# VectorE's order around the masked rows of the second graph

## Chip, cores and metric

One core of a Trainium2 chip runs the kernel. The metric is the device time of one execution in microseconds (us). Three runs of the kernel before gave 1057.75, 1055.41 and 1055.34 us, median 1055.41.

## The reference

For 32 batches `x` (256 channels by 512 nodes) two graph layers follow each other, each with a residual and a layer norm:

- Layer 0: two projections of `x` give a query and a key for each node; the softmax of the leaky ReLU of their sums is the attention; `agg = x @ att^T`, then `relu(adj @ agg + bias)`, added to `x`, and a layer norm over the last axis gives `h`.
- Layer 1, on rows of `h`: `z_l = h W_lang^T` and `z_g = h W_grav^T`. One 256 by 256 matrix is `A_l = max(zn zn^T, 0)` with normed rows `zn`, without its diagonal; the other is `A_g = exp(-d2 / 2 sigma^2)` with the squared distances of the rows of `z_g`. `adj` stands as the mask of both: `K_l = A_l * mask / row sums`, `K_g` likewise. `out = (w K_l + (1 - w) K_g) (h W_V^T) W_O^T`, added to `h`, and a second layer norm.

## The kernel before

The 32 batches are taken in 16 pairs. A step of the main loop has three pairs in flight: layer 1 of pair p, layer 0 of pair q = p + 1, and the projections of `x` (the x products) of pair r = p + 2. Two set-up steps come first (`early`); in the last two of the sixteen main steps no new pair comes in (`new` is false). Every engine has its own program, in which the order of the work is written out by hand, and the engines meet at semaphores only: `wait_ge` holds the engine, and all that stands behind it in its program, until a count is reached.

Matrices are kept as two float16 parts, `_hi` (made by ACT, a rounded copy) and `_lo` (made by VectorE or GpSimd, what the rounding left), and each product is three matmuls per 128 rows of contraction: hi by hi, hi by lo, lo by hi (L254 to L256). Products go to eight PSUM banks.

The part of a step that the change touches runs as follows.

- TensorE (`step`, from L509): x products 0, 1 and 2 (`wx_product`), into banks 0, 1 and 2; then `add_transposed(0)` and `(1)`, sixteen matmuls of 128 columns that add the transposed halves of the language similarity in banks 4 and 5; `norm_rows`, which spreads the inverse norms of the rows over bank 3 (semaphore `r_mm`); x products 3, 4 and 5, again into banks 0, 1 and 2; `add_transposed(2)`; x products 6 and 7 (banks 0 and 1); `add_transposed(3)`; the value products `v_product(0)` (bank 2), `(1)` (bank 0) and `(2)` (bank 1), `turn_k` for both batches, `v_product(3)` and the output products.
- An x product from the fourth on waits until the bank is read: `wx_product(k)` waits for `xw_lo` tile k - 3 (L504). Likewise `v_product(0)` waits for xw_lo tile 5, `(1)` for tile 6 and `(2)` for tile 7 (L453).
- ACT copies each x product to `xw_hi` (L616) as soon as it is there.
- VectorE makes `xw_lo` of each tile (`xw_lo_tile`: a copy of two columns at L909, then a subtraction of 256 columns at L910), and among these tiles it does other work in a fixed order: after tiles 0, 1 and 2 comes `t_lo_tile(3)` (L1069); then `masked_rows`, which for both batches of the pair multiplies the rows of bank 3 by the mask, two operations of 256 columns for each (L1102); then xw_lo tiles 3, 4 and 5; then `a_l_tiles` (L1111), which multiply the masked rows by the similarity and sum them up; `a_g_tile`, tiles 6 and 7, the sums of degrees and the K tiles (L1139).
- GpSimd makes the `h_lo` tiles (L1272) after `t_lo_tile(3)`, and SP sends them through a transposing DMA for the next step.

Of the kernel before, what the change touches and what calls it, by code (L numbers as in the profile page):

```python
# [27 lines left out]
ALU = mybir.AluOpType  # L28
# [23 lines left out]
def build(nc, x, adj, adjT, wqk, bm, wl, wg, wv, woT, gate, sigma, out):  # L52
# [4 lines left out]
    CC, OC, NC, DC = C // P, O // P, N // P, D // P  # L57
# [5 lines left out]
    with ExitStack() as ctx:  # L63
        def sb(name, shape, dt=F32):
            return ctx.enter_context(nc.sbuf_tensor(name, [P, *shape], dt))

        def sem(name):
            return ctx.enter_context(nc.semaphore(name))
# [6 lines left out]
        mask = sb("mask", [OC, O])  # L75
# [50 lines left out]
        a_l, a_g = sb("a_l", [2, OC, O]), sb("a_g", [2, OC, O])  # L126
# [13 lines left out]
        halves = [b[:].rearrange("p (c n) -> p c n", c=2) for b in bank]  # L140
# [9 lines left out]
        def wx_bank(p, k):  # L150

            return bank[late[k % 4] if p < 0 else k % 3]
# [31 lines left out]
        s = {n: sem(n) for n in names}  # L184
# [582 lines left out]
        def _(dve):  # L767
# [138 lines left out]
            def xw_lo_tile(p, k):  # L906
                r = p + 2
                dve.wait_ge(s["xw_hi_done"], 8 * r + k + 1)
                dve.tensor_copy(qk[:, k, :], wx_bank(p, k)[:, O:OW])  # L909
                dve.tensor_tensor(xw_lo[:, k // NC, k % NC, 0:O], wx_bank(p, k)[:, 0:O],  # L910
                                  xw_hi[:, k // NC, k % NC, 0:O], ALU.subtract).then_inc(s["xw_lo_done"], 1)
# [124 lines left out]
            def step(p, l0, new):  # L1036
# [28 lines left out]
                def t_lo_tile(k):  # L1065
                    dve.wait_ge(s["t_hi_done"], 4 * p + k + 1)
                    if k >= 2:
                        dve.wait_ge(s["shift_done"], 2 * p + k - 1)
                    dve.scalar_tensor_tensor(out=t_lo[:, k], in0=halves[4 + k] if k < 2 else a_g[:, k - 2],  # L1069
                                             scalar=2.0 ** -6, in1=t_hi[:, k],  # L1070
                                             op0=ALU.mult, op1=ALU.subtract).then_inc(s["t_lo_done"], 1)
# [23 lines left out]
                                                        accum_out=deg_g[:, k:k + 1])  # L1095
                    last.then_inc(s["ag_done"], 1)

                def masked_rows():
                    dve.wait_ge(s["r_mm"], p + 1)
                    for j in range(2):  # L1100
                        for c in range(OC):
                            last = dve.tensor_tensor(a_l[:, j, c, :], halves[3][:, j, :], mask[:, c, :], ALU.mult)  # L1102
                        last.then_inc(s["mr_done"], 1)

                def a_l_tiles():
                    for k in range(4):

                        j, c = k // 2, k % 2
                        dve.wait_ge(s["s_mm"], 4 * p + j + 1)
                        dve.wait_ge(s["mr_done"], 2 * p + j + 1)  # L1110
                        last = dve.scalar_tensor_tensor(out=a_l[:, j, c, :], in0=halves[4 + j][:, c, :], scalar=0.0,  # L1111
                                                        in1=a_l[:, j, c, :], op0=ALU.max, op1=ALU.mult,
                                                        accum_out=deg_l[:, k:k + 1])
                    last.then_inc(s["al_done"], 1)
# [103 lines left out]
                if new:  # L1218
                    for k in range(3):
                        xw_lo_tile(p, k)  # L1220
                t_lo_tile(3)
                masked_rows()
                if new:
                    for k in range(3, 6):
                        xw_lo_tile(p, k)
                a_l_tiles()
                a_g_tile(0)
                if new:
# [16 lines left out]

            setup0()
            pipeline(step)
            for k in range(4):
                o_stat_tile(PAIRS - 1, k)
# [107 lines left out]
```

## Time and profile before

| what | value |
|---|---|
| profiled execution, its own time | 1057.68 us |
| its span | 1056.0 us |
| median of the three runs | 1055.41 us |
| TensorE busy | 1022.2 us (97%) |
| VectorE busy | 793.9 us (75%) |
| ACT busy | 658.3 us (62%) |
| GpSimd busy | 386.2 us (37%) |
| mean granted TensorE clock | 0.991 |

The profile records one execution, the one of 1057.68 us; the span is the part of it that the instructions take. Busy time counts from the start to the end of each instruction. Matmuls are pipelined and their ends are modelled, so the distance between starts says more of TensorE than its busy time does. An instruction's row shows when it started, how long it took, and, where its engine stood idle before it, for how long and whose work ended that.

### The profile page before, as it was taken

The numbers are of one execution on the slowest core, as the hardware profiler recorded it, in microseconds if no ns is written. First come the engines' busy times: TensorE is split into PE (matmuls) and PEld (weight loads), VectorE is DVE, ScalarE is ACT, GpSimd is POOL, SyncE is SP. The second block draws the span as 40 slices with busy tenths as digits, with TensorE's granted clock in tenths as the row PEclk, the third lists the DMA queues.
The fourth block names the chain that finished last, engine by engine and source line by source line (L and its number), as shares of the span: only waits on it lengthen the run. The fifth ranks groups of instructions, "written<-read, shape, count | busy, mean of one in ns | idle before, by whom it ended". The sixth has DMA issues, their size and how long they took to land.

```text
span 1056.0 us, 19673 instructions
## 1 busy us (share of the span) xinstructions
PE 1022.2 (97%) x7189; PEld 697.6 (66%) x7189; DVE 793.9 (75%) x2318; ACT 658.3 (62%) x1267; POOL 386.2 (37%) x340
## 2 busy tenths in 40 slices
PE   7988999999999999999999999999999999999995
PEld 4464848667584866758486775848677584857662
DVE  4776677868877786887778687777868777786766
ACT  2657566675766667575666757576675757666432
POOL 0334325163442516344251625425162542515200
PEclk9998999999999999999999999999999999999998
DMA  7010131413123141312314130231413023131211
GB/s 264 35 61 20 21 101 41 121 41 81 41 61 100 41 120 41 84 39 61 101 41 121 41 89 33 61 100 41 120 41 88 34 61 100 41 80 41 41 41 41
DMA packets 85233, 72.05 MB, mean 68 GB/s; under 512 B 64144, under 2 KB 64656, under 8 KB 83088
## 3 DMA queue, kind: packets, MB, share of 16 engines
q1 hardware_dynamic: 85136, 70.79, 23.0%
q8 instruction: 57, 0.93, 0.4%
q14 instruction: 40, 0.33, 0.1%
HBM read 21.50 MB, written 16.78 MB: 36 GB/s over the span
## 4 chain that ended last, share of the span: by engine, by line
PE 69%; DVE 9%; ACT 7%; issue 6%; POOL 1%; POOLq 0%; DVEq 0%; ACTq 0%
PE bank L254 21%; PE bank L256 21%; PE bank L255 21%; ACT t_hi L671 3%; PE bank L338 3%; ACT a_g L666 2%; DVE t_lo L1069 2%; DVE a_l L1102 2%; PE bank L261 1%; DVE h L968 1%; DVE xw_lo L910 1%; ACT att_hi L700 1%; PE bank L478 1%; DVE vb L1054 1%; DVE vb L1077 1%
## 5 line engine op out<-in xcount | busy, mean ns | idle before, releaser
L1289 POOL TENSOR_TENSOR att_lo<-att,att_hi 128x512 f16<-128x512 f32 x128 | 148.5, 1160 | 346.9 <-ACT att_hi L584 346.9
L254 PE MATMUL bank<-xw_hi,att_hi 128*128 128x257 f16 x512 | 140.4, 274 | 1.2 <-DVE wvo_lo L858 1.0
L254 PE MATMUL bank<-ht_hi,z_hi 128*128 128x256 f16 x512 | 139.6, 273 | 0.0
L255 PE MATMUL bank<-ht_lo,z_hi 128*128 128x256 f16 x512 | 139.6, 273 | 0.0
L256 PE MATMUL bank<-ht_hi,z_lo 128*128 128x256 f16 x512 | 139.6, 273 | 0.0
L256 PE MATMUL bank<-xw_hi,att_lo 128*128 128x257 f16 x512 | 139.4, 272 | 0.0
L255 PE MATMUL bank<-xw_lo,att_hi 128*128 128x257 f16 x512 | 139.1, 272 | 0.0
L1043 DVE TENSOR_TENSOR z_lo<-bank,z_hi 128x512 f16<-128x512 f32 x128 | 88.2, 689 | 48.7 <-ACT z_hi L655 48.7
L603 ACT ACTIVATE agg_t<-bank,den_inv 128x256 f32<-128x256 f32 x128 | 58.8, 473 | 80.3 <-DVE den_inv L903 79.9
L1272 POOL TENSOR_TENSOR att_lo<-h,att_hi 128x512 f16<-128x512 f32 x60 | 67.7, 1159 | 102.4 <-DVE t_lo L1069 102.4
L683 ACT ACTIVATE z_hi<-bank 128x512 f16<-128x512 f32 x64 | 37.9, 596 | 101.4 <-PE bank L256 99.5
L254 PE MATMUL bank<-wvo_hi,ht_hi 128*128 128x512 f16 x256 | 97.0, 379 | 0.0
L255 PE MATMUL bank<-wvo_lo,ht_hi 128*128 128x512 f16 x256 | 97.0, 379 | 0.0
L256 PE MATMUL bank<-wvo_hi,ht_lo 128*128 128x512 f16 x256 | 97.0, 379 | 0.0
L938 DVE SCALAR_TENSOR_TENSOR att<-a_row,u_col,bank 128x512 f32<-128x512 f32 x120 | 88.7, 739 | 9.8 <-POOL att_lo L1289 7.2
L584 ACT ACTIVATE att_hi<-att 128x512 f16<-128x512 f32 x128 | 80.2, 627 | 22.9 <-DVE att L938 22.9
L655 ACT ACTIVATE z_hi<-bank 128x512 f16<-128x512 f32 x128 | 75.1, 586 | 23.0 <-PE bank L256 23.0
L578 ACT ACTIVATE bank<-b_row,v_col 128x512 f32<-128x512 f32 x120 | 80.7, 681 | 1.2
L254 PE MATMUL bank<-wm_hi,x_hi 128*128 128x258 f16 x256 | 71.3, 278 | 9.2 <-DVE xw_lo L910 6.9
L1303 POOL TENSOR_TENSOR y<-y,x_res 128x512 f32<-128x512 f32 x32 | 47.1, 1472 | 89.0 <-ACT y L610 88.9
L256 PE MATMUL bank<-wm_hi,x_lo 128*128 128x258 f16 x256 | 70.6, 276 | 0.0
L616 ACT ACTIVATE xw_hi<-bank 128x256 f16<-128x256 f32 x128 | 45.7, 382 | 39.9 <-PE bank L256 39.9
(177 smaller groups left out, 2660.3 us busy)
## 6 DMA issues: line engine op xcount, KB each, us to landing
x_in<-in_x SPq DMA_DIRECT2D x16, 1024.0 KB, 5.4
x_res<-x_in SPq DMA_DIRECT2D x16, 1024.0 KB, 5.2
out_y<-o SPq DMA_DIRECT2D x32, 512.0 KB, 2.9
agg_t<-in_wl SPq DMA_DIRECT2D x4, 256.0 KB, 3.9
y<-in_wg SPq DMA_DIRECT2D x1, 1024.0 KB, 10.1
o<-in_wv SPq DMA_DIRECT2D x1, 1024.0 KB, 12.3
h<-in_woT SPq DMA_DIRECT2D x1, 1024.0 KB, 14.4
att<-in_adjT SPq DMA_DIRECT2D x1, 256.0 KB, 3.7
```

The costliest lines, as they stand in the source:

```text
L254: pe.matmul(dst, ah, bh, start=(i == 0 and first), stop=False, skip_group_check=skip)
L255: pe.matmul(dst, ah, bl, start=False, stop=False, skip_group_check=skip)
L256: last = pe.matmul(dst, al, bh, start=False, stop=(i == n - 1), skip_group_check=skip)
L578: act.activation(vb_of(q, g), b_row[:, j, :], ACT.Copy, scale=v_col[:, j, n:n + 1])\
L584: act.activation(att_hi[:, g // NC, g % NC, :], att[:, g % 2, :], ACT.Copy)\
L603: act.activation(agg_t[:, k // NC, k % NC, :], bank[k % 4][:, 0:O], ACT.Copy, scale=den_inv[:, k:k + 1]).then_inc(s["agg_done"], 1)
L655: act.activation(z_hi[:, g, :], bank[g % 4][:], ACT.Copy).then_inc(s["z_hi_done"], 1)
L938: dve.scalar_tensor_tensor(out=att[:, g % 2, :], in0=a_row[:, j, :], scalar=u_col[:, j, n:n + 1], in1=vb_of(q, g), op0=ALU.mult, op1=ALU.max)\
L1043: dve.tensor_tensor(z_lo[:, g, :], bank[g % 4][:], z_hi[:, g, :], ALU.subtract)\
L1272: pool.tensor_tensor(h_lo[:, k, :], h_of(q)[:, k, :], h_hi[:, k, :], ALU.subtract)\
L1289: pool.tensor_tensor(att_lo[:, n[0], n[1], :], att[:, g % 2, :], att_hi[:, n[0], n[1], :], ALU.subtract).then_inc(s["att_lo_done"], 1)
L1303: pool.tensor_tensor(y[:, k, :], y[:, k, :], x_res[:, k // 2, k % 2, :], ALU.add)\
```

## The change

`masked_rows` takes the batch of the pair as its argument `j` and does two operations instead of four. It is called once ahead of xw_lo tiles 3 and 4 and once behind them. Each call waits for `r_mm` (already met at the second); the count on `mr_done` is as before, one for each batch. In the two last steps, without a new pair, the two calls follow each other, as the four operations did.

```diff
-                def masked_rows():
+                def masked_rows(j):
                     dve.wait_ge(s["r_mm"], p + 1)
-                    for j in range(2):
-                        for c in range(OC):
-                            last = dve.tensor_tensor(a_l[:, j, c, :], halves[3][:, j, :], mask[:, c, :], ALU.mult)
-                        last.then_inc(s["mr_done"], 1)
+                    for c in range(OC):
+                        last = dve.tensor_tensor(a_l[:, j, c, :], halves[3][:, j, :], mask[:, c, :], ALU.mult)
+                    last.then_inc(s["mr_done"], 1)
...
                 t_lo_tile(3)
-                masked_rows()
-                if new:
-                    for k in range(3, 6):
-                        xw_lo_tile(p, k)
+                masked_rows(0)
+                if new:
+                    xw_lo_tile(p, 3)
+                    xw_lo_tile(p, 4)
+                masked_rows(1)
+                if new:
+                    xw_lo_tile(p, 5)
                 a_l_tiles()
```

## Rows read from the trace of the kernel before

**Rows 1.** Page, part 1: busy us, share of the span and instructions of each engine.

```profile
PE 1022.2 (97%) x7189; PEld 697.6 (66%) x7189; DVE 793.9 (75%) x2318; ACT 658.3 (62%) x1267; POOL 386.2 (37%) x340
```

**Rows 2.** Waits of TensorE: who waited for whom, us in total, times, longest us.

```profile
PE bank L254 <- DVE xw_lo L910: 6.9, 16, 1.4
```

**Rows 3.** Windows: us, then busy us (x instructions) by engine, PEclk, DMA share, GB/s.

```profile
180.00:200.00 20.00, 19.63 (x162) 14.35 (x161) 16.85 (x72) 12.81 (x29) 6.03 (x6) 1.00 0.42 104
200.00:220.00 20.00, 20.00 (x103) 10.23 (x102) 15.41 (x25) 15.02 (x28) 5.63 (x5) 1.00 0.17 56
```

**Rows 4.** Timeline of TensorE, 190 to 193 us: start, duration, instruction [idle before <- releaser].

```profile
190.30 0.22 PE L446 MATMUL bank<-ident,t_lo 128*128 128x128 f16 x1
190.88 0.28 PE L254 MATMUL bank<-wm_hi,x_hi 128*128 128x258 f16 x1 [0.37 <-DVE xw_lo L910]
191.56 0.27 PE L254 MATMUL bank<-wm_hi,x_hi 128*128 128x258 f16 x1
...
192.61 0.22 PE L446 MATMUL bank<-ident,t_lo 128*128 128x128 f16 x1
192.67 0.38 PE L254 MATMUL bank<-wvo_hi,ht_hi 128*128 128x512 f16 x1
```

**Rows 5.** Timeline of VectorE, 188 to 198 us.

```profile
188.43 0.68 DVE L1069 SCALAR_TENSOR_TENSOR t_lo<-a_g,t_hi 128x512 f16<-128x512 f32 x1
189.02 1.41 DVE L1102 TENSOR_TENSOR a_l<-bank,mask 128x256 f32<-128x256 f32 x4
190.35 0.15 DVE L909 COPY qk<-bank 128x2 f32<-128x2 f32 x1
190.42 0.41 DVE L910 TENSOR_TENSOR xw_lo<-bank,xw_hi 128x256 f16<-128x256 f32 x1
...
191.21 0.41 DVE L910 TENSOR_TENSOR xw_lo<-bank,xw_hi 128x256 f16<-128x256 f32 x1
191.55 0.41 DVE L1111 SCALAR_TENSOR_TENSOR a_l<-bank,a_l 128x256 f32<-128x256 f32 x1
...
193.68 0.41 DVE L910 TENSOR_TENSOR xw_lo<-bank,xw_hi 128x256 f16<-128x256 f32 x1
...
196.83 1.67 DVE L1139 SCALAR_TENSOR_TENSOR a_l<-a_g,s_g,a_l 128x256 f32<-128x256 f32 x4
```

**Rows 6.** Timeline of ACT in the same stretch, xw_hi tiles 3 and 4.

```profile
188.78 0.38 ACT L616 ACTIVATE xw_hi<-bank 128x256 f16<-128x256 f32 x1 [1.05 <-PE bank L256]
189.45 0.38 ACT L616 ACTIVATE xw_hi<-bank 128x256 f16<-128x256 f32 x1 [0.28 <-PE bank L256]
```

**Rows 7.** Timeline of TensorE, later: second value product, turn_k, next step.

```profile
195.26 0.38 PE L254 MATMUL bank<-wvo_hi,ht_hi 128*128 128x512 f16 x1
...
200.44 1.04 PE L478 MATMUL bank<-ident,a_l 128*128 128x128 f32 x8
...
210.17 0.38 PE L254 MATMUL bank<-ht_hi,ul_hi 128*128 128x512 f16 x1
```

**Rows 8.** GpSimd's timeline, and the DMA issues with median us to landing.

```profile
189.18 4.51 POOL L1272 TENSOR_TENSOR att_lo<-h,att_hi 128x512 f16<-128x512 f32 x4 [6.90 <-DVE t_lo L1069]
...
ht_lo<-att_lo SPq DMA_TRANSPOSE x15, 4.4
```

**Rows 9.** Timeline of TensorE: a wait in set-up, first and last of 14 in steps.

```profile
71.68 0.27 PE L254 MATMUL bank<-wm_hi,x_hi 128*128 128x258 f16 x1 [1.36 <-DVE xw_lo L910]
...
129.42 0.28 PE L254 MATMUL bank<-wm_hi,x_hi 128*128 128x258 f16 x1 [0.36 <-DVE xw_lo L910]
...
928.78 0.28 PE L254 MATMUL bank<-wm_hi,x_hi 128*128 128x258 f16 x1 [0.37 <-DVE xw_lo L910]
```

**Rows 10.** Timeline of VectorE and TensorE in the step that lost most.

```profile
435.19 1.41 DVE L1102 TENSOR_TENSOR a_l<-bank,mask 128x256 f32<-128x256 f32 x4
...
436.32 0.22 PE L446 MATMUL bank<-ident,t_lo 128*128 128x128 f16 x1
437.05 0.28 PE L254 MATMUL bank<-wm_hi,x_hi 128*128 128x258 f16 x1 [0.51 <-DVE xw_lo L910]
```

## The prediction

> **What bounds the kernel now.** I read four views. The page's busy shares come first: TensorE is busy 1022.2 of 1056.0 us, VectorE 793.9 [rows 1]. So the end is set by TensorE, and a VectorE edit that adds and removes no instruction can only be worth a pause of TensorE. The table of TensorE's waits comes next: one line stands out, 16 waits of L254 (the first matmul of a product) on the `xw_lo` tiles, 6.9 us [rows 2]. The table by windows shows the form of it: the 20 us around one of these waits have 19.63 us of TensorE, the next 20 us have 20.00, and the granted clock is 1.00 in both, its 2.4 GHz level [rows 3]. Last the timeline of one step. Between the eighth matmul of the third `add_transposed` (start 190.30) and the first of x product 6 (start 190.88) lie 0.58 us, where the same change from 128-column matmuls to a product at 192.61 to 192.67 takes 0.06 [rows 4]. TensorE loses 0.52 us there, once in a step of 61.46 us (129.42 to 190.88 [rows 4, 9]); the full 20.00 us of the window behind it show no second pause like it.
>
> The 0.37 us that the waits view gives for this pause counts from the modelled end of the matmul before, and those ends overlap (0.22 us long, 0.05 to 0.06 apart). I take the distance of starts. The Trainium skill (Perfetto Trace Analysis, "Summary: the profiler window per engine type") says of TensorE that the shown end of an instruction is estimated; by that the starts are the better measure, and the trace agrees in that matmuls start before the one ahead has ended. By the waits view's idle time the sum below would be 5.3 us (13 times 0.37 and once 0.51), by the starts 7.4.
>
> **What the pause waits for.** x product 6 needs bank 0, and `wx_product(6)` waits until xw_lo tile 3 has read it. VectorE does t_lo tile 3 (188.43), four masked rows (189.02) and then tile 3: copy 190.35, subtraction 190.42 for 0.41 us, so done 190.83, and TensorE goes 0.05 later [rows 4, 5]. ACT's part of tile 3 was done at 188.78 + 0.38 = 189.16 [rows 6]: it is not what is waited for. VectorE has no idle time between 188.43 and 191.55, so tile 3 is late because of what is queued ahead of it.
>
> **The change, part by part.** Nothing is added or removed but one wait of VectorE on `r_mm`, which the first half has already met; no DMA, no other engine's program and no queue is edited.
>
> *Two of the four masked rows go behind tiles 3 and 4.* The four take 190.35 - 189.02 = 1.33 us of VectorE, 0.333 each [rows 5], so tile 3 moves 0.67 us ahead: copy at 189.69, done at 190.17, TensorE free to go at 190.22. The matmuls themselves would let product 6 start at 190.30 + 0.06 = 190.36. The pause of 0.52 goes whole, with 0.14 to spare.
>
> *What is late next.* Tile 4, one tile of 0.40 us later (190.42 to 191.21 are two), is done at 190.57; product 7, 0.68 after product 6 (190.88 to 191.56), would start at 191.04 and needs it by 190.99: 0.42 spare. ACT's part of tile 4 is done at 189.45 + 0.38 = 189.83, and VectorE asks for it at 190.09: 0.26 spare. The second half of the masked rows then stands ahead of tile 5, which comes out where it was, 191.21 + 0.41 = 191.62, since the same instructions lie ahead of it; `v_product(0)` needs its bank and would start at 192.67 - 0.52 = 192.15: 0.48 spare [rows 4 to 6]. Tile 6 ends at 194.09 as before, `v_product(1)` would start at 195.26 - 0.52 = 194.74: 0.60 spare. `turn_k(0)` would start at 199.92 and its four K tiles end at 198.50: 1.4 spare [rows 5, 7].
>
> *The cost of the moved rows* is nothing: the a_l tiles that read them start at 191.55 either way. The cover is those spare times; if it were gone, each 0.1 us costs 14 times 0.1 = 1.4 us. *The new transitions*: once more a masked row follows a subtraction and a copy follows a masked row. No row shows the first. From below they cost nothing (the pitch of 0.333 holds for four in a row and from the masked rows to the copy); from above 0.08 each, if the overlap of a row of 0.41 with the next were lost. I take nothing, as the nearest rows show; even twice 0.08 lies inside the spare times but for product 6, where one comes (masked row to copy, which the trace has), 0.14 - 0.08. *The extra wait* is already met: below nothing; above the 0.07 us between a copy and its subtraction. I take nothing, since every copy has a wait of its own and still follows in 0.33 us.
>
> *DMA.* GpSimd's h_lo tiles wait for t_lo tile 3, which keeps its place: 189.18 for 4.51 us, then the transpose of 4.4 us median, so landed near 198.1; the next step begins at 210.17 and would begin 0.52 earlier [rows 7, 8]. All else that crosses into the next step (the K rows, the residual) follows TensorE and moves with it.
>
> **The sum.** The change acts in steps with a new x pair, 14 of 16; the trace has 14 such pauses, from 129.42 to 928.78, the idle time 0.36 or 0.37 us in 13 and 0.51 in one [rows 9]. The other two waits of the sixteen belong to the set-up (71.68 is one), which is not edited. In the odd step the starts are 436.32 and 437.05, so 0.73 - 0.06 = 0.67 us lost; there tile 3 would be done at 435.19 + 0.67 + 0.07 + 0.41 = 436.34 and the product could go at 436.39 against 436.38 by the matmuls [rows 10]: 0.66 gained. Together 13 x 0.52 + 0.66 = 7.4 us. Against the profiled execution's own 1057.68 us this is 1050.3. That execution lies with the slowest of the three runs shown (1057.75); the two others are 1055.34 and 1055.41. From the median, 1055.41 - 7.4 = **1048.0 us**, and an execution like the profiled one would read 1050.3.
>
> **Rivals.**
>
> *The pause moves on to the next bank.* The three banks of the x products rotate and tile 5 is not a nanosecond earlier. For it: VectorE is back to back from 188.43 to 191.55 [rows 5], so whatever TensorE gains it gains against an engine that does not get faster. Against: the 0.48 and 0.60 us worked out above. If TensorE stops at `v_product(0)` for all of the 0.52, nothing is gained: 1055.4. The Trainium skill (Perfetto Trace Analysis, "Optimization Strategy") reads a gap that repeats on the busiest engine as a possible lack of buffers, so one that a new order could not cure; the wait on bank 0 agrees with that, the spare times at banks 1 and 2 do not.
>
> *Half of it.* Tile 3's 0.14 us of spare is the thinnest. If transitions, wait and a later ACT copy together cost VectorE 0.4 us ahead of tile 3, 0.26 of 0.52 remains to be gained: 14 x 0.26 = 3.6 us, 1051.8.
>
> *Slower.* Before, the masked rows are work that VectorE can do while ACT copies tiles 3 and 4. Behind them, if ACT's tile 4 comes late, VectorE stands, and behind it stand two masked rows, tile 5, the a_l tiles and `degrees`. It decides from where ACT's copy of tile 4 ends: after 189.83 + 0.26 + 0.42 = 190.51 product 7 starts late and the gain shrinks, after 191.03 (0.52 more) it is a loss. Half a microsecond past that point, 0.5 x 14 = 7 us, gives 1062.4. For it: ACT stands directly between the product and the tile. Against: copies 3 and 4 follow their products at once, and the odd step among the 14 lost 0.15 us more than the others, not 1.2.
>
> *The change does not do what it says* would need tile 3 to wait for ACT; 189.16 against 189.69 excludes it by 0.53.
>
> **How the numbers follow.** The forecast 0.85; the pause moved to the next bank 0.04; half of it 0.08; slower 0.03. What a measurement of this kernel can tell from no change is 0.3%, 3.2 us: the forecast is faster in either of the two levels the runs show (1048.0 or 1050.3), half of it is on the line (half counted on each side), the moved pause is the same. So faster 0.89, same 0.08, slower 0.03. The range takes the forecast with 1 us below it (13 pauses read to 0.01, and the 0.15 us of the odd step), the level of the profiled execution and most of the half: 1046.8 to 1051.8.
>
> **What would show it.** In the changed kernel's trace the waits of TensorE on xw_lo fall from 16 to 2, about 1.6 us; the start of product 6 follows the last `add_transposed` matmul by 0.06 us; masked rows appear in two pairs of about 0.74 us with two tiles between; tile 5 keeps its place against t_lo tile 3; steps of 60.94 instead of 61.46 us. The prediction is wrong if a new wait stands at `v_product(0)` or `turn_k(0)`, if VectorE is idle ahead of tile 4's copy, or if the steps shorten but the total does not.

## The result: 9 us faster, 1.6 us below the forecast

| | before | after |
|---|---|---|
| median of 6 runs | 1055.54 us (1054.95 to 1057.75) | 1046.39 us (1044.92 to 1047.79) |
| profiled execution, span | 1057.68, 1056.0 us | 1045.15, 1043.4 us |
| ratio after to before | | 0.9913, interval 0.9902 to 0.9923 |

The forecast was 1048.0 us, its range 1046.8 to 1051.8: the direction was right, and the time came out 0.4 us below the range. One execution of all those on record, of the kernel with all four rows behind tile 5, read 1340.64 us at a mean granted clock of 0.752 and is left out of every comparison.

The mechanism first. TensorE's waits on `xw_lo` (who waited for whom, us in total, times, longest us) are down from the sixteen of [rows 2] to the two of the set-up:

```profile
PE bank L254 <- DVE xw_lo L910: 1.6, 2, 1.4
```

TensorE's timeline of the step (start, duration, instruction) has the answer to [rows 4]: the eighth matmul of `add_transposed(2)`, x products 6 and 7, the end of `add_transposed(3)` and the first matmul of the first value product.

```profile
184.90 0.22 PE L446 MATMUL bank<-ident,t_lo 128*128 128x128 f16 x1
184.96 0.27 PE L254 MATMUL bank<-wm_hi,x_hi 128*128 128x258 f16 x1
...
185.62 0.27 PE L254 MATMUL bank<-wm_hi,x_hi 128*128 128x258 f16 x1
...
186.68 0.22 PE L446 MATMUL bank<-ident,t_lo 128*128 128x128 f16 x1
186.73 0.38 PE L254 MATMUL bank<-wvo_hi,ht_hi 128*128 128x512 f16 x1
```

Product 6 follows by 0.06 us where it was 0.58, and `v_product(0)` by 0.05: nothing took the place of the wait. VectorE in the same stretch, against [rows 5]:

```profile
183.02 0.68 DVE L1069 SCALAR_TENSOR_TENSOR t_lo<-a_g,t_hi 128x512 f16<-128x512 f32 x1
183.62 0.74 DVE L1101 TENSOR_TENSOR a_l<-bank,mask 128x256 f32<-128x256 f32 x2
184.28 0.15 DVE L909 COPY qk<-bank 128x2 f32<-128x2 f32 x1
184.35 0.41 DVE L910 TENSOR_TENSOR xw_lo<-bank,xw_hi 128x256 f16<-128x256 f32 x1
...
185.08 0.74 DVE L1101 TENSOR_TENSOR a_l<-bank,mask 128x256 f32<-128x256 f32 x2
...
185.81 0.41 DVE L910 TENSOR_TENSOR xw_lo<-bank,xw_hi 128x256 f16<-128x256 f32 x1
186.14 0.41 DVE L1110 SCALAR_TENSOR_TENSOR a_l<-bank,a_l 128x256 f32<-128x256 f32 x1
```

Two pairs of masked rows, tile 3 done at 184.76, and tile 5 in its old place: 2.79 us behind t_lo tile 3, before 2.78. The step is read from the start of its first matmul: 143.31, 204.24, 265.16 and so on to 935.53, so 60.93 us where it was 61.47; the odd step went from 61.77 to 61.10. The two rows below are the second and the last of these starts, 12 steps and 731.29 us apart.

```profile
204.24 0.38 PE L254 MATMUL bank<-ht_hi,ul_hi 128*128 128x512 f16 x1
...
935.53 0.38 PE L254 MATMUL bank<-ht_hi,ul_hi 128*128 128x512 f16 x1
```

In the kernel before the same 12 steps run from 210.17 [rows 7] to the row below, 737.90 us:

```profile
948.07 0.38 PE L254 MATMUL bank<-ht_hi,ul_hi 128*128 128x512 f16 x1
```

The difference, 6.61 us, is eleven steps of 0.54 and the odd one of 0.67; with the pauses of the first two of the 14 steps it is 13 x 0.54 + 0.67 = 7.7 us. But the two profiled spans lie 1056.0 - 1043.4 = 12.6 us apart. The other 4.9 us are in the set-up and in the first main step, ahead of the instructions that the change moves. In windows (us, busy us by engine with instructions, granted clock, DMA) first before, then after: the set-up, and the first main step.

```profile
0.00:78.60 78.60, 64.93 (x336) 42.86 (x337) 50.11 (x147) 35.60 (x77) 19.35 (x24) 0.96 0.35 118
78.60:148.70 70.10, 65.63 (x452) 43.64 (x453) 48.04 (x137) 45.76 (x88) 23.39 (x19) 0.95 0.21 57
```

```profile
0.00:75.70 75.70, 62.36 (x336) 41.40 (x337) 50.02 (x147) 35.58 (x77) 19.33 (x24) 0.98 0.36 124
75.70:143.30 67.60, 62.51 (x452) 43.07 (x453) 47.79 (x137) 45.17 (x88) 23.38 (x19) 1.00 0.22 57
```

The same instructions took 2.9 us less in the set-up, and 2.5 us less in the first step, of which 0.54 is the pause. The granted clock was lower before, in both. A second thing differs in the set-up, and the clock does not show it: when the first loads land. VectorE's first work on them, before, after, and in the next trace of the changed kernel:

```profile
9.65 0.69 DVE L790 TENSOR_REDUCE top_part<-att 128x1 f32<-128x512 f32 x1 [7.56 <-DMA knobs<-in_sigma]
```

```profile
8.20 0.69 DVE L790 TENSOR_REDUCE top_part<-att 128x1 f32<-128x512 f32 x1 [6.12 <-DMA knobs<-in_sigma]
```

```profile
9.83 0.69 DVE L790 TENSOR_REDUCE top_part<-att 128x1 f32<-128x512 f32 x1 [7.74 <-DMA knobs<-in_sigma]
```

The first x product of the set-up starts at 15.76, 14.49 and 15.94 us in these three, so 1.27 of the 2.9 us are there before it. In the third the set-up is 1.5 us longer than in the second at the same mean clock, 0.996, and 1.45 of that stand ahead of the first x product. So a pair of executions can differ by 4.9 us ahead of the first instruction that the change moves; what is in question is whether the medians' 9.15 us against 7.7 is that.

### The profile page after: what moved, and what is told of

It reads as the page before. It is cut to its first block, busy times and chain, and to the rows that moved or that the text cites. A ratio compares the mean times of both kernels' runs of the same rounds, so it can differ in the third digit from the quotient of the medians.

```text
span 1043.4 us, 19673 instructions
## 1 busy us (share of the span) xinstructions
PE 1014.2 (97%) x7189; PEld 695.5 (67%) x7189; DVE 792.3 (76%) x2318; ACT 654.6 (63%) x1267; POOL 385.6 (37%) x340
## 4 chain that ended last, share of the span: by engine, by line
PE 84%; issue 5%; DVE 1%; ACT 1%; POOL 1%; POOLq 0%; DVEq 0%; ACTq 0%
PE bank L254 25%; PE bank L255 25%; PE bank L256 25%; PE bank L338 3%; PE bank L446 2%; PE bank L261 2%; PE bank L478 1%; POOL att_lo L1274 0%; DVE o L896 0%; ACT bank L578 0%; DVE t_lo L1069 0%; ACT t_hi L671 0%; ACT a_g L666 0%; ACT z_hi L655 0%; POOLq L63 0%
## 5 line engine op out<-in xcount | busy, mean ns | idle before, releaser
L255 PE MATMUL bank<-ht_lo,z_hi 128*128 128x256 f16 x512 | 139.6, 273 | 0.0
L255 PE MATMUL bank<-xw_lo,att_hi 128*128 128x257 f16 x512 | 139.1, 272 | 0.0
L1274 POOL TENSOR_TENSOR att_lo<-h,att_hi 128x512 f16<-128x512 f32 x60 | 67.6, 1159 | 102.3 <-DVE t_lo L1069 102.3
L255 PE MATMUL bank<-wvo_lo,ht_hi 128*128 128x512 f16 x256 | 97.0, 379 | 0.0
L255 PE MATMUL bank<-wm_lo,x_hi 128*128 128x258 f16 x256 | 69.8, 273 | 0.0
```

What stands on the lines that cost most here:

```text
L255: pe.matmul(dst, ah, bl, start=False, stop=False, skip_group_check=skip)
L1274: pool.tensor_tensor(h_lo[:, k, :], h_of(q)[:, k, :], h_hi[:, k, :], ALU.subtract)\
```

## The experiments

Theory A: the change is worth the pause at bank 0, 7.7 us (7.6 in the expectations below is the same sum), and what the times show beyond is the set-up, which varies from one execution to the next. Theory B: the program as changed also shortens the set-up, always. And of the pause: its size follows from the VectorE work ahead of tile 3, with the spare times that the prediction worked out.

**The split in place.**

```diff
                 masked_rows(0)
+                masked_rows(1)
                 if new:
-                    xw_lo_tile(p, 3)
-                    xw_lo_tile(p, 4)
-                masked_rows(1)
-                if new:
-                    xw_lo_tile(p, 5)
+                    for k in range(3, 6):
+                        xw_lo_tile(p, k)
```

> The masked rows in two calls with a wait each, but both calls ahead of tiles 3 to 5, so the order of the kernel before with the changed kernel's function. Theory A: steps of 61.46 us with the wait on xw_lo at product 6 (14 waits of about 0.37 us), time of the kernel before within 0.1%. Theory B (it is the split, the added wait or the changed layout of the program that speeds up the set-up): 1.5 to 2.5 us faster than before with steps of 61.46 us.

Measured 1055.58 us beside 1055.91 (ratio 0.9995, 0.9982 to 1.0007), steps of 61.47 us, the waits as before:

```profile
PE bank L254 <- DVE xw_lo L910: 6.9, 16, 1.4
```

The steps are those of before, and the interval of the times holds 1: no effect of the split and the second wait is seen. Its profiled execution happened to have the short set-up, and that gives the cleanest pair:

```profile
0.00:75.90 75.90, 62.51 (x336) 41.51 (x337) 49.95 (x147) 35.60 (x77) 19.36 (x24) 0.98 0.36 123
75.90:144.10 68.20, 62.74 (x453) 43.10 (x454) 47.90 (x137) 45.46 (x88) 23.41 (x19) 1.00 0.21 57
```

Set-up 75.9 against 75.7 us, first step 68.2 against 67.6, span 1051.3 against 1043.4: 7.9 us, 0.2 of it set-up and 7.7 the steps. The order of before gets the short set-up too.

**The changed kernel again**, twice.

> The changed kernel itself, timed again beside the kernel before. What is open: its trace shows steps of 60.93 us against 61.46 (14 steps, 13 x 0.54 + 0.67 = 7.6 us), its times are 9.15 us lower (1055.54 to 1046.39). Theory A: the change is worth the 7.6 us of the steps, the rest is the set-up ahead of the first changed instruction, which comes out up to 5 us apart from one execution to the next; then a second set of runs gives 7 to 9 us and the first main step can read 64.6 or 66.5 us in either kernel. Theory B: the changed program also makes the set-up or the first step shorter, always; then again 9 to 10 us and a first step of 64.6 us.

> The changed kernel a third time, for the 1.5 us by which its times gained more than its steps. Theory A: runs of before and after with the same mean granted clock (0.995 and above: set-up with one stretch at 1.2 GHz; 0.992 and below: with three) differ by 7 to 8 us, and the rest is which of the two set-ups an execution happens to get, so the changed kernel's share of the longer set-up can be anything from a quarter to two thirds. Theory B (the changed program always has the shorter set-up): all six runs at 0.994 or above.

Measured 1046.61 beside 1055.91 us (0.9914, 0.9898 to 0.9929) and 1047.33 beside 1055.37 (0.9922, 0.9909 to 0.9934): 9.3 and 8.0 us, steps of 60.93 us each. The 9.3 lies above the 7 to 9 us of theory A and within the 9 to 10 of theory B. The first main steps of the two traces are as short as in the first trace of the changed kernel, so they do not tell the theories apart either:

```profile
77.10:144.80 67.70, 62.56 (x453) 43.12 (x454) 47.89 (x137) 45.30 (x88) 23.42 (x19) 1.00 0.22 59
```

```profile
76.10:143.80 67.70, 62.58 (x453) 43.12 (x454) 47.83 (x137) 45.28 (x88) 23.37 (x19) 1.00 0.22 59
```

From the second main step to the end all three traces of the changed kernel take 900.1 us, those of the kernel before and of the split in place 907.3: what varies within a kernel lies ahead of it. Theory B as it was put for the third set falls: two of its five executions read a clock of 0.990 (1048.38 and 1048.64 us). That the set-up is shorter on average is not excluded by this. All 17 executions of the changed kernel, and the 26 of the kernel before in these two sets, sorted by their mean clock:

| mean granted clock | before | after | difference of medians |
|---|---|---|---|
| 0.995 and above | 5, median 1054.18 | 8, median 1046.19 | 8.0 us |
| 0.993 and 0.994 | 7, median 1055.52 | 4, median 1047.05 | 8.5 us |
| 0.992 and below | 14, median 1056.75 | 5, median 1047.85 | 8.9 us |

Theory A expected 7 to 8 us at like clock. The group of the high clock has 8.0, the others 8.5 and 8.9, so 0.3 to 1.2 us over the steps' 7.7 remain, and no run tells what they are. The sorting is rough: the mean clock says nothing of when the loads landed, and the trace of the kernel with TensorE's order changed (below) began its second main step at 144.80 us with a clock of 0.991, the one with all four rows behind at the same 144.80 with 0.995. The changed kernel got the high clock in 8 of 17, the one before in 5 of 26, which moves the medians further apart (the split in place, with the order of before, had it in 5 of 12).

**One row behind instead of two.** The rows are written one by one here: `masked_rows(j)` is `masked_row(j, 0)` and `masked_row(j, 1)`.

```diff
                 masked_row(0, 0)
                 masked_row(0, 1)
+                masked_row(1, 0)
                 if new:
                     xw_lo_tile(p, 3)
                     xw_lo_tile(p, 4)
-                masked_row(1, 0)
                 masked_row(1, 1)
```

> Three masked rows ahead of tiles 3 and 4, one behind. Theory A (tile 3 alone decides, each row ahead of it costs 0.333 us): tile 3 comes 0.33 us earlier, 0.19 to 0.20 us of pause stay, steps of 61.13 us, 14 x 0.33 + 0.13 = 4.8 us faster than before. The rival that the pause depends on another thing (ACT's copy, the first row alone): steps of 61.46 or 60.93 us.

Measured 1051.29 us (0.9958, 0.9943 to 0.9974), steps of 61.13 us. At product 6 TensorE loses 0.25 - 0.06 = 0.19 us:

```profile
249.03 0.22 PE L446 MATMUL bank<-ident,t_lo 128*128 128x128 f16 x1
249.28 0.28 PE L254 MATMUL bank<-wm_hi,x_hi 128*128 128x258 f16 x1
```

One row is worth 0.333 us a step, as reckoned. The list of waits has this pause only for the odd step: in the others the product starts 0.03 us after the modelled end of the matmul ahead, and no idle time is put down.

**Tile 3 late, and tile 5 late.** One spare operation ahead of tile 3; in another kernel two ahead of tile 5.

```diff
                 masked_rows(0)
                 if new:
+                    spare_row(0)
                     xw_lo_tile(p, 3)
                     xw_lo_tile(p, 4)
```

```diff
                 masked_rows(1)
                 if new:
+                    spare_row(0)
+                    spare_row(1)
                     xw_lo_tile(p, 5)
```

> The changed kernel with one more operation of a masked row's size (its result is not used) between the first pair and tile 3. By the changed kernel's trace product 6 has 0.15 us to spare, so theory A expects 0.18 us of pause and steps of 61.11 us, 2.6 us slower than the changed kernel. If VectorE's order no longer mattered: 60.93 us; with no spare time: 61.26 us.

> The changed kernel with two more operations of a masked row's size (their result is not used) behind the second pair and ahead of tile 5: tile 5 comes 0.67 us later. By the changed kernel's trace v_product(0) has 0.46 us to spare, so theory A expects it 0.21 us late and steps of 61.14 us (14 x 0.21 = 2.9 us slower than the changed kernel). If the spare time were larger than reckoned: 60.93 us; if there were none: 61.60 us.

Measured 1050.18 us (0.9950, 0.9936 to 0.9964) with steps of 61.13, and 1050.78 us (0.9956, 0.9942 to 0.9969) with steps of 61.15. Product 6 with tile 3 late, then `v_product(0)` with tile 5 late (one more line in the file, so L255):

```profile
248.96 0.22 PE L447 MATMUL bank<-ident,t_lo 128*128 128x128 f16 x1
249.21 0.28 PE L255 MATMUL bank<-wm_hi,x_hi 128*128 128x258 f16 x1
```

```profile
250.40 0.22 PE L447 MATMUL bank<-ident,t_lo 128*128 128x128 f16 x1
250.67 0.39 PE L255 MATMUL bank<-wvo_hi,ht_hi 128*128 128x512 f16 x1
```

0.33 us ahead of tile 3 cost 0.19: 0.14 was spare, the prediction's number. 0.67 ahead of tile 5 cost 0.21: 0.46 was spare, where 0.48 was worked out. The next bank in the rotation was free in time because of this half microsecond and not by any rule.

**All four rows behind tile 5.**

```diff
-                masked_rows(0)
                 if new:
-                    xw_lo_tile(p, 3)
-                    xw_lo_tile(p, 4)
-                masked_rows(1)
-                if new:
-                    xw_lo_tile(p, 5)
+                    for k in range(3, 6):
+                        xw_lo_tile(p, k)
+                masked_rows(0)
+                masked_rows(1)
```

> All four masked rows behind tiles 3, 4 and 5. Theory A: with no pause left in the step there is nothing more to gain: steps of 60.93 us and the time of the changed kernel, since the matmuls follow each other without a gap; tile 3 waits for ACT instead (its copy ends 0.53 us before the changed kernel asks for it), which would leave VectorE idle for about 0.1 us ahead of tiles 4 and 5 and cost nothing. The rival (VectorE's order is still what ends last in the step): steps shorter than 60.93 us by up to 0.3 us. The rival that idle VectorE time is paid behind (K tiles late): steps longer than 60.93 us.

Measured 1050.41 us, the median of five executions (0.9950, 0.9931 to 0.9969), steps of 61.09 us: slower than the changed kernel by 0.16 us a step, and the "cost nothing" of theory A was wrong. VectorE:

```profile
184.52 0.68 DVE L1069 SCALAR_TENSOR_TENSOR t_lo<-a_g,t_hi 128x512 f16<-128x512 f32 x1
185.30 0.16 DVE L909 COPY qk<-bank 128x2 f32<-128x2 f32 x1
...
185.96 0.16 DVE L909 COPY qk<-bank 128x2 f32<-128x2 f32 x1 [0.17 <-ACT xw_hi L616]
...
186.62 0.16 DVE L909 COPY qk<-bank 128x2 f32<-128x2 f32 x1 [0.17 <-ACT xw_hi L616]
...
187.03 1.41 DVE L1101 TENSOR_TENSOR a_l<-bank,mask 128x256 f32<-128x256 f32 x4
188.35 0.41 DVE L1110 SCALAR_TENSOR_TENSOR a_l<-bank,a_l 128x256 f32<-128x256 f32 x1
...
190.49 0.42 DVE L910 TENSOR_TENSOR xw_lo<-bank,xw_hi 128x256 f16<-128x256 f32 x1
```

Tiles come every 0.66 us, ACT's pace, not 0.40: VectorE waits, and the a_l tiles start 3.83 us behind t_lo tile 3 where it was 3.12. Of these 0.7 us, what the spare time does not cover is paid at `v_product(1)`, which needs tile 6, done at 190.91 (the last matmul of `v_product(0)`, then the first of `v_product(1)`):

```profile
190.60 0.38 PE L256 MATMUL bank<-wvo_hi,ht_lo 128*128 128x512 f16 x1
190.96 0.39 PE L254 MATMUL bank<-wvo_hi,ht_hi 128*128 128x512 f16 x1
```

0.36 where matmuls of 512 columns follow each other in 0.22: 0.14 of the step's 0.16 us. This is the prediction's "slower" rival in small: the masked rows between the tiles are what VectorE does while ACT copies.

**The pause filled from TensorE's side**, with VectorE's order of before.

```diff
                 add_transposed(2)
+                add_transposed(3)
                 if new:
                     wx_product(6)
                     wx_product(7)
-                add_transposed(3)
-                if new:
                     v_product(0)
```

> VectorE's order of the kernel before; TensorE does add_transposed(3) ahead of x products 6 and 7, not behind them, so that its 0.45 us fill most of the pause. Theory A (what is gained is the pause at bank 0, whichever engine's order removes it): 0.08 us of pause stay, steps of 61.02 us, 6.2 us faster than before. The rival (it is VectorE's order that shortens the step): steps of 61.46 us.

Measured 1049.33 us (0.9941, 0.9927 to 0.9954), steps of 61.01 us; product 6 starts 0.13 behind `add_transposed(3)`, 0.07 of it lost:

```profile
247.86 0.22 PE L446 MATMUL bank<-ident,t_lo 128*128 128x128 f16 x1
247.99 0.28 PE L254 MATMUL bank<-wm_hi,x_hi 128*128 128x258 f16 x1
```

So it is the pause at bank 0 that is worth the time, from whichever side it is closed.

**Steps against times.** For each kernel, the gain over 14 steps read from its trace, and that of the medians of its own set:

| kernel | 13 steps + the odd one | steps, us | medians, us |
|---|---|---|---|
| one row behind | 13 x 0.34 + 0.33 | 4.7 | 4.6 |
| tile 5 late | 13 x 0.32 + 0.62 | 4.8 | 4.6 |
| tile 3 late | 13 x 0.34 + 0.64 | 5.1 | 5.2 |
| all behind | 13 x 0.38 + 0.52 | 5.5 | 5.5 |
| TensorE's order | 13 x 0.46 + 0.46 | 6.4 | 6.0 |
| the change | 13 x 0.54 + 0.67 | 7.7 | 9.15, 9.3, 8.0 |

None of these kernels beats the changed one, and in its trace nothing of the pause is left to gain.

## Why the prediction was wrong, and where it was right

- *What bounds the kernel; what the pause waits for; the two rows move tile 3.* Right, and shown: half the move gives 0.333 us a step, all of it 0.54, and closing the pause from TensorE's side gives nearly the same.
- *What is late next.* Right in order and size: 0.14 and 0.46 us of spare time measured against 0.14 and 0.48.
- *New transitions and the added wait cost nothing.* Right: tile 5 keeps its place within 0.01 us, and the split alone changes no step.
- *The sum, 13 x 0.52 + 0.66 = 7.4.* The steps gave 13 x 0.54 + 0.67 = 7.7. The missing 0.02 is the product behind the pause: its second matmul came 0.13 us after the first, now 0.11. The waits view's 5.3 would have been 2.4 us short.
- *The base and the edge of the range* are the step that failed. "1 us below it (13 pauses read to 0.01, and the 0.15 us of the odd step)" allowed for my reading and not for the two sets of runs that would be compared: the prediction put the difference of the set-ups at nothing, since the set-up "is not edited". I took three runs as two levels, and forecast from the median with only the higher one as an alternative. Later sets have the kernel before between 1052.83 and 1057.86 us, and the changed one between 1044.92 and 1048.64, while from the second main step on the traces of either kernel agree to 0.1 us. The medians of three sets lie 0.5 us apart before and 0.9 after. Of the 1.6 us below the forecast, 0.3 are the sum's, and the median of six, 0.1 above that of three, takes 0.1 back: the steps' 7.7 off 1055.54 give 1047.8, and 1046.39 is 1.4 lower.
- *What stays open:* the cause of that 1.4 us (1.6 and 0.3 in the other two sets). Two things are seen to vary ahead of the second main step, the granted clock and the landing of the first loads; that they make up the medians' 1.4 us is not shown. That the changed program always gets the high clock is excluded, no such effect of the split alone is seen, and five related kernels agree with their steps within 0.4 us. But all three sets of the changed kernel gained more than its steps, where none of the five others did by more than 0.2 us, and it had the high clock oftener. No run tells whether that is more than luck.
- *Rivals.* The pause did not move on, nor did half of it stay. The slower one did not come; its mechanism is real, as all four rows behind tile 5 show, though it is paid at `v_product(1)` and tile 6, not at product 7 as I had it. The Trainium skill (Perfetto Trace Analysis, "Optimization Strategy") takes a gap that repeats as a possible lack of buffers; the trace here does not agree, since the distance of starts went from 0.58 to 0.06 us with the same three banks.

## What to carry to other kernels

Where TensorE is the bound, look for the one place in the step where its starts are too far apart, find the bank it waits for, and ask which work ahead of the bank's reader could as well stand behind it; then work out the spare time at each later wait before moving more, since a row too many behind the tiles leaves VectorE waiting for ACT. Judge such a change by the length of the step in the trace, which repeats to 0.01 us here, and give the forecast of the total the spread of the part that does not repeat.

## What the runs showed of the hardware

The granted clock of the same stretch, with the same work, differs between executions. Three windows of 5 us in the first main step, before and then after, which start at like places of the step:

```profile
85.00:90.00 5.00, 2.15 (x10) 0.60 (x7) 2.32 (x4) 4.92 (x11) 1.16 (x1) 1.00 0.00 0
90.00:95.00 5.00, 3.74 (x10) 1.11 (x11) 3.63 (x6) 4.63 (x10) 3.47 (x3) 0.58 0.00 0
95.00:100.00 5.00, 5.00 (x19) 2.00 (x18) 4.22 (x7) 4.41 (x9) 3.52 (x4) 0.73 0.01 2
```

```profile
82.10:87.10 5.00, 2.13 (x10) 0.60 (x7) 2.35 (x4) 4.92 (x11) 1.16 (x1) 1.00 0.00 0
87.10:92.10 5.00, 2.78 (x13) 1.11 (x14) 3.63 (x6) 4.63 (x10) 3.47 (x3) 1.00 0.00 0
92.10:97.10 5.00, 5.00 (x33) 3.02 (x31) 4.19 (x7) 4.53 (x10) 3.55 (x4) 1.00 0.01 2
```

TensorE was busy for 2.15 and 2.13 of 5 us, pausing 2.57 us for `z_lo` in both; behind that one execution fell to the 1.2 GHz level for part of two windows (0.58 and 0.73 on the mean) and the other stayed at 2.4. It cost some 1.9 us by the first step: 2.5 less the 0.54 of the pause. The split in place, with the order of before and a clock of 1.00 in that step, took 68.2 us for it against 70.1. Nor do the first loads land at the same time: the work that waits for them started at 8.20, 9.65 and 9.83 us in the three rows shown with the result, and the first x product at 14.49, 15.76 and 15.94.
